# One router pass for both token tiles of a batch in the small experts of a four-layer model

## The reference

```python
logits = xf @ Wgate + expert_bias            # 8 experts
probs = jax.nn.softmax(logits, axis=-1)
topk_p, topk_i = jax.lax.top_k(probs, K)     # K = 2
topk_p = topk_p / jnp.sum(topk_p, axis=-1, keepdims=True)
comb = jnp.sum(jax.nn.one_hot(topk_i, E, dtype=xf.dtype) * topk_p[..., None], axis=1)
routed = jnp.einsum('ne,nec->nc', comb, _experts(xf, Wg, Wu, Wd))
return (shared + routed).reshape(b, t, c)
```

## Time and profile before

| | |
|---|---|
| time, median of 3 runs | 1422.37 us (1421.27 to 1424.42) |
| the profiled execution | 1424.82 us, span 1423.0 us |
| TensorE busy | 1323.8 us, 93% |
| VectorE busy | 1005.4 us, 71%, 1516 instructions |
| ScalarE busy | 871.2 us, 61% |
| POOL busy | 400.2 us, 28% |
| mean granted TensorE clock | 0.981 |

### The profile page before, as it was taken

How to read it: one execution, slowest core, us unless ns; L and a number is a source line. 1 busy time by engine, 2 the same in 40 slices (tenths; PEclk the granted TensorE clock), 3 DMA queues, 4 the chain that set the end, 5 groups by cost and what they waited for, 6 DMA issues and landing times.

```text
span 1423.0 us, 27091 instructions
## 1 busy us (share of the span) xinstructions
PE 1323.8 (93%) x10934; PEld 562.0 (39%) x10934; DVE 1005.4 (71%) x1516; ACT 871.2 (61%) x1104; POOL 400.2 (28%) x331
## 2 busy tenths in 40 slices
PE   7999998889879999999999998989998999999997
PEld 5344333333324444333444343433433334433443
DVE  3534777889925347698887868688868697978735
ACT  3334347788784454276566767666768676675672
POOL 5554430110011755452220223022305033202010
PEclk8999999999999999999999999999999999999998
DMA  6633101000001731011111010110010101100100
GB/s 177 118 62 70 25 14 31 16 2 2 2 1 39 196 60 34 1 32 24 35 24 24 1 23 1 24 35 10 15 24 1 23 13 24 31 13 19 24 1 15
DMA packets 30291, 45.80 MB, mean 32 GB/s; under 512 B 5892, under 2 KB 10692, under 8 KB 30116
## 3 DMA queue, kind: packets, MB, share of 16 engines
q1 hardware_dynamic: 30168, 44.08, 14.0%
HBM read 25.39 MB, written 1.18 MB: 19 GB/s over the span
## 4 chain that ended last, share of the span: by engine, by line
PE 72%; DVE 11%; ACT 8%; issue 4%; SPq 3%; DMA 2%; POOL 0%; ACTq 0%; DVEq 0%
PE ps L1264 13%; PE ps L1364 11%; PE ps L1309 7%; ACT PR L1442 6%; PE ps L1230 5%; PE ps L1250 5%; PE ps L1231 5%; PE ps L1232 5%; DVE BM L1530 3%; PE ps L1844 3%; PE ps L1328 2%; PE ps L1242 2%; PE ps L1271 2%; PE ps L1375 2%; PE ps L1324 1%
## 5 line engine op out<-in xcount | busy, mean ns | idle before, releaser
L1442 ACT ACTIVATE PR<-ps 128x1024 f32<-128x1024 f32 x432 | 431.2, 1026 | 207.1 <-PE ps L1271 136.4
L1530 DVE TENSOR_REDUCE BM<-ps 128x2 f32<-128x1024 f32 (+2 forms) x384 | 350.4, 950 | 57.0 <-PE ps L1250 55.9
L1264 PE MATMUL ps<-QS,KS 48*128 48x512 f16 (+7 forms) x2688 | 306.1, 329 | 31.7 <-ACT PR L1442 22.5
L1364 PE MATMUL ps<-PR,VS 128*32 128x512 f32 (+3 forms) x2304 | 231.5, 499 | 2.2 <-ACT PR L1442 1.6
L1264 PEld LDWEIGHTS ps<-QS,KS 48*128 48x128 f16 (+1 forms) x2688 | 108.5, 95 | 203.6 <-ACT PR L1442 88.5
L1250 PE MATMUL ps<-KS,QS 48*128 48x128 f16 (+2 forms) x1728 | 161.7, 273 | 19.2 <-DVE BM L1530 10.8
L1523 DVE TENSOR_REDUCE BM<-ps 128x8 f32<-128x1024 f32 x96 | 116.8, 1220 | 39.3 <-PE ps L1250 38.5
L1250 PEld LDWEIGHTS ps<-KS,QS 48*128 48x128 f16 x1728 | 68.0, 94 | 135.3 <-issue 45.8
L1571 POOL TENSOR_TENSOR OS<-OS,RX 128x512 f32<-128x512 f32 x24 | 30.5, 1270 | 273.9 <-ACT RX L1458 273.9
L1230 PE MATMUL ps<-YA,QS 128*128 128x512 f16 x256 | 99.6, 389 | 0.8 <-DVE RX L1489 0.5
L1231 PE MATMUL ps<-YA,QS 128*128 128x512 f16 x256 | 99.2, 388 | 0.0
(11 more groups left out here) (299 smaller groups left out, 2054.9 us busy)
## 6 DMA issues: line engine op xcount, KB each, us to landing
PR<-gates SPq DMA_DIRECT2D x32, 512.0 KB, 12.5
QS<-KS SPq DMA_DIRECT2D x64, 128.0 KB
QS<-KS SPq DMA_DIRECT2D x64, 64.0 KB
WM<-W_in SPq DMA_DIRECT2D x1, 2048.0 KB, 9.0
QS<-HL SPq DMA_DIRECT2D x48, 32.0 KB
KS<-HL SPq DMA_DIRECT2D x48, 32.0 KB
QS<-CT SPq DMA_DIRECT2D x96, 2.0 KB
KS<-KS SPq DMA_DIRECT2D x8, 128.0 KB, 2.4
```

Source lines behind the costliest of these rows:

```text
L1264: ins = pe.matmul(ps[pair][:, w, off:off + cols], KS[rows, ks, kt * P:(kt + 1) * P], QS[rows, qs, (ph + 1) * TT - cols:(ph + 1) * TT], sta ...
L1364: ins = pe.matmul(dst[32 * j:32 * j + 32, TT - cols:TT], v, PR[:, buf, j, off:off + cols], start=(g == 0), stop=(g == NGRP[ph] - 1))
L1442: act.activation(dst, src, ACT.Exp, scale=0.125 if lat else 1.0).then_inc(sig["exp"], 1)
L1530: ins = dve.tensor_reduce(BM[:, ph, p, :, qt - 4 * ph, part], bnk[:, :, off:off + nk * P], AX.X, ALU.max)
```

## The change

`routed(r, t)` says which tiles share a router: both of a batch, but for the second layer's batch 1 (r = 3, tiles 2 and 3), where each stays alone. `lg` now waits for the normalised rows of both tiles and issues 8 matmuls, the 22 steps and the exponential work on 64 columns (8 small ones), and only the transposes and all that follows stay a tile at a time. The step buffers move: six in `wq0`, four in `goon`, the bf16 parts in `gT`, the small columns in `ohb`, all of which an earlier router has left free. The planner's costs are 2.2 instead of 1.1 us for a shared `lg` and 0.23 instead of 0.20 us for a shared step. Five constants leave the priority tables with the values they had. The order of every engine in `Late` is laid out anew from these tasks with the same priorities.

```diff
         for t in (2 * b, 2 * b + 1):
             before = self.tile_before(r, t)
-            q = add("PE", f"lg{b}", ("lg", r, t), ("scl", kn, t), ("gtr",) + before if before else None)
-            for j in range(ROUTE):
-                x = add("DVE", f"rt{b}", ("rt", r, t, j), ("rt", r, t, j - 1) if j else q,
-                        ("rex", r, t) if j == 13 else None)
-                if j == 0:
-                    self.take(q, "misc", x)
-                if j == 2:
-                    add("ACT", f"rex{b}", ("rex", r, t), x)
-            q = add("PE", f"gtr{b}", ("gtr", r, t), x, ("gs",) + before + (1,) if before else None)
+            tiles = self.routed(r, t)
+            if t == tiles[0]:
+                x = add("PE", f"lg{b}", ("lg", r, t), *[("scl", kn, i) for i in tiles], ("gtr",) + before if before else None)
+                for j in range(ROUTE):
+                    q, x = x, add("DVE", f"rt{b}", ("rt", r, t, j), x, ("rex", r, t) if j == 13 else None)
+                    if j == 0:
+                        self.take(q, "misc", x)
+                    if j == 2:
+                        add("ACT", f"rex{b}", ("rex", r, t), x)
+                gates = x
+            q = add("PE", f"gtr{b}", ("gtr", r, t), gates, ("gs",) + before + (1,) if before else None)
...
+    def routed(r, t):
+
+        return (t,) if (r, t // 2) == (3, 1) else (t // 2 * 2, t // 2 * 2 + 1)
...
+        if task[0] in ("lg", "rt"):
+            n = len(self.routed(*task[1:3]))
+            return 1.1 * n if task[0] == "lg" else 0.17 + 0.03 * n
...
-        RTV = [wq0[:, :, :].rearrange("p n m -> p (n m)")[:, 32 * i:32 * i + 32] for i in range(10)]
-        RTB = wq0[:, :, :].rearrange("p n m -> p (n m)")[:, 320:368].bitcast(BF16).rearrange("p (i c) -> p i c", i=4)
+        RTV = ([wq0[:, :, :].rearrange("p n m -> p (n m)")[:, 64 * i:64 * i + 64] for i in range(6)]
+               + [goon[:, 64 * i:64 * i + 64] for i in range(4)])
+        RTB = gT[:, 0:96].bitcast(BF16).rearrange("p (i c) -> p i c", i=KT)
         GTB = rt_more[:, 0:256].bitcast(BF16)
-        RTM = [rt_more[:, 256 + 4 * i:256 + 4 * i + 4] for i in range(5)]
+        RTM = [ohb[:, :].bitcast(F32)[:, 8 * i:8 * i + 8] for i in range(5)]
...
-                    pe.wait_ge(sig["scl"], c("scl", 4 * (r - 1), t))
-                    for i in range(4):
+                    for i in range(4 * len(Late.routed(r, t))):
+                        if i % 4 == 0:
+                            pe.wait_ge(sig["scl"], c("scl", 4 * (r - 1), t + i // 4))
                         ins = pe.matmul(one[:, i * E:(i + 1) * E], XN[:, t * TT + i * P:t * TT + (i + 1) * P], w_rt1,
                                         start=True, stop=True)
...
-                    pe.wait_ge(sig["rt"], c("rt", r, t, ROUTE - 1))
+                    pe.wait_ge(sig["rt"], c("rt", r, Late.routed(r, t)[0], ROUTE - 1))
```

More of the change, by code:

```diff
@@ L265, in priority @@
         if kind == "sc":
-            v = None if scores >= w["scm"] else w["sc"] + w["sc1"] * scores
+            v = None if scores >= 2 else w["sc"] + w["sc1"] * scores
         elif kind == "un":
             lead = self.lead()
-            v = None if units >= w["unm"] or lead > w["leadm"] else (w["un0"] if lead <= w["lead"] else w["un2"]) + w["un1"] * units - w["une"] * (self.at["eu"][1] < 63)
+            v = None if units >= 2 or lead > 4 else (w["un0"] if lead <= w["lead"] else w["un2"]) + w["un1"] * units - w["une"] * (self.at["eu"][1] < 63)
         elif kind == "pv":
@@ L476 @@
              "SP": ("gd", "egb", "crow", "put", "kput", "st", "wl1", "wl2")}
[L477 to L480, removed]
+    WISH = {"sc": 2, "sc1": 1.02, "un0": 1.9, "un2": 2.1, "lead": 2, "un1": 1, "une": 1, "pv3": 2.5, "ahead": 3,
+            "pv": 3.61, "qk": 0.71, "vl": 1.9, "proj": 3.06, "ed": 1.1, "mean": 1, "eu": 1.2, "eu1": 0.3,
+            "mode": 0.4, "bldf": 0.8, "bld2": 3.31, "bld": 1.8, "up": 1.7, "dn": 1.22, "short": 1}
     def build(self):
@@ L681, in priority @@
                 first = task[1] in FAST
-                if (m > w["bldm"] and not first) or held >= (2 if first else 1):
+                if (m > 2 and not first) or held >= (2 if first else 1):
                     return None
@@ L686, in priority @@
                 held = sum(1 for x in self.held.values() if x[0] == "up")
-                return None if held >= w["upm"] and self.at["sc"][1] < 2 * NN - 1 else w["up"]
+                return None if held >= 2 and self.at["sc"][1] < 2 * NN - 1 else w["up"]
             return w["dn"] if kind in ("dn", "val") else w["short"]
@@ L1813, in pe_late @@
                     r, t = args
-                    pe.wait_ge(sig["rt"], c("rt", r, t, ROUTE - 1))
+                    pe.wait_ge(sig["rt"], c("rt", r, Late.routed(r, t)[0], ROUTE - 1))
                     pe.wait_ge(s_zero, ZERO[1] + 1)
                     for i in range(4):
-                        ins = pe.matmul(one[0:24, i * P:(i + 1) * P], RTB[:, i, :], onesb[:, :], start=True, stop=True)
+                        ins = pe.matmul(one[0:24, i * P:(i + 1) * P], RTB[:, 4 * (t - Late.routed(r, t)[0]) + i, :], onesb[:, :], start=True, stop=True)
                     ins.then_inc(sig["gtr"], 1)
@@ L1933, in act_late @@
                     act.wait_ge(sig["rt"], c("rt", r, t, 2))
-                    act.activation(RTV[1], RTV[0], ACT.Exp).then_inc(sig["rex"], 1)
+                    n = 4 * E * len(Late.routed(r, t))
+                    act.activation(RTV[1][:, 0:n], RTV[0][:, 0:n], ACT.Exp).then_inc(sig["rex"], 1)
                 elif kind == "gwh":
@@ L2002, in v3, with route, over_e @@
                 return x.rearrange("p (i e) -> p i e", e=E)
-            def over_e(x):
-                return x.unsqueeze(2).to_broadcast([P, 4, E])
-            first_choice = desc[:, :].unsqueeze(1).to_broadcast([P, 4, E])
-            def route(j, logits):
-                v = [v3(x) for x in RTV]
+            def route(j, logits, n):
+                def over_e(x):
+                    return x.unsqueeze(2).to_broadcast([P, n, E])
+                v = [v3(x[:, 0:n * E]) for x in RTV]
+                m = [x[:, 0:n] for x in RTM]
+                parts = RTB[:, 0:n, :]
+                first_choice = desc[:, :].unsqueeze(1).to_broadcast([P, n, E])
                 if j == 0:
-                    return dve.tensor_tensor(v[2], logits[:, 0:4 * E].rearrange("p (i e) -> p i e", e=E),
-                                             brow[:, :].unsqueeze(1).to_broadcast([P, 4, E]), ALU.add)
+                    return dve.tensor_tensor(v[2], logits[:, 0:n * E].rearrange("p (i e) -> p i e", e=E),
+                                             brow[:, :].unsqueeze(1).to_broadcast([P, n, E]), ALU.add)
                 if j == 1:
-                    return dve.tensor_reduce(RTM[0], v[2], AX.X, ALU.max)
+                    return dve.tensor_reduce(m[0], v[2], AX.X, ALU.max)
                 if j == 2:
-                    return dve.tensor_tensor(v[0], v[2], over_e(RTM[0]), ALU.subtract)
+                    return dve.tensor_tensor(v[0], v[2], over_e(m[0]), ALU.subtract)
                 if j == 3:
```

25 lines of the change are left out of this document (14 added, 11 removed), and 3 rows, old and new, of the table WISH.

## The result

The changed kernel took 1429.92 us (median of 12 executions, 1423.66 to 1432.55), the kernel before 1422.15 us beside it (12 executions, 1419.05 to 1429.04). The ratio is 1.0043, 95% interval 1.0025 to 1.0061: slower by 0.43%, where I had forecast 0.3% faster. The profiled execution took 1431.99 us, with a span of 1430.2 us.

A forecast was written before the change was run, and what follows sets the result against it. TensorE, busy 93%, was taken as the bound, so only its waits for VectorE counted: -6.0 + 2.2 = -3.8, about -4 us, from the median 1422.4 to 1418.4 us. The range was 1413 to 1427, the likeliest case 1416 to 1420.5.

The forecast's parts named there:

- 66 instructions, 12.1 us: VectorE's router instructions fall from 176 to 110; 66 removed at 0.184 us each, 12.1 us of busy time.
- The waits as the direct gain, -6.0: TensorE's waits for VectorE in three router windows (1.85, 1.84, 2.29 us), all taken as given back: -6.0 us.
- The widening, +2.2: The 66 router instructions in merged passes go from 32 to 64 columns, 34 ns each: at most 2.2 us added.
- The moved gates, 0 (between -4 and +4): Tile 0's gates and down projection, some 55 us later, fill idle time or displace attention: -4 to +4, taken as 0.
- The chain of the batch, 5.4 us late, covered: Tile 1's down projection ends 5.4 us later, puts 2.2 and 4.7 us late; cost 0, up to 6.9 if uncovered.
- the cover: Next quad's row of maxima is issued by 974.3, attention before it ends at 992.94: 18 us to hide late puts.
- Slower: Both tiles' gates meet in one bunch and the new order feeds TensorE worse: +5, 1427.4 us; chance 0.28.
- Its test: Idle and clock together, from router's start to second down projection, over 4 us more a batch than before.
- The order laid out anew: Planner's new order feeds TensorE worse around the gates: one more bad window +2, two +8; within Slower's 0.28.

The follow-up runs named there:

- e2_late: Kernel before, routers still separate, but tile 0's logits wait for tile 1's normalised rows in the three merged pairs, order laid out anew; ratio 1.0008.
- narrow form of the change: Changed kernel, same order and eight logits matmuls a pair, but a merged pass's steps and exponential work on tile 0's 32 columns alone; ratio 1.0006.
- draw: Kernel before, separate routers, with one planner cost altered so the order is laid out anew; three such kernels measured 1.0099, 1.0040 and 1.0161.
- pass in two halves: Changed kernel, same order, but each merged VectorE step issued as two of the old width, one a tile; ratio 1.0063, 1434.1 us.
- e7_merged_order_a: Changed kernel with only the planner's cost of a router step 0.01 larger, putting 526 TensorE tasks at another place; ratio 1.0006.

## Why the prediction was wrong, step by step

**66 instructions, 12.1 us.** Right: 1450 instead of 1516, 11.6 us less busy.

**The waits as the direct gain, -6.0.** This is the step that failed first. I took every wait of TensorE for VectorE in a window where a router runs as the router's doing. Leaving 54 steps out left the waits of all three windows where they were and gave +0.3 us (-3 to +4) at the order of before; at the late order +0.0006 against e2_late. The term was 0.

**The widening, +2.2.** The duration was right: 222 ns against 188 is the 34 ns that I worked out. The price was wrong by place. Charged in full it was still 2.2 us, as if time on VectorE were the most that it could cost. It cost nothing that can be told where a router stands early, about 5 us (1 to 9) at the change's order and about 10 (5 to 16) at the late one, there with four more logits matmuls a pair. All of the first and most of the second came as a lower granted clock of TensorE. In these two places a longer pass ahead of the gates was followed by more half-speed time; I had priced the wait and not what follows it. With 0 for the first term and 5 us for this one, my sum gives +5, near the measured +6.1 us (1.0043).

**The moved gates, 0 (between -4 and +4).** Right as a sum: 1.0008 with late gates alone. In the narrow form of the change, though, it is a balance: +6.2 us of rest and -5.8 of clock part, both clear of their errors (with late gates alone +3.8 and -1.9, the second not clear). The change so stands as late gates and a new order that cost some 6 us of stalls and would give as much back in clock, and a width that takes this back.

**The chain of the batch, 5.4 us late, covered.** Wrong in sign in two of the three batches, and without consequence: the merged pass started 3 us earlier than tile 1's router had and let tile 1's down projection begin at 820.98 instead of 827.53; in the second batch it began 1.7 us earlier, in the third 0.3 us later. The two puts went out 0.5 and 3.5 us later than before. TensorE's waits for transfers behind the first start are the same three as before, 1.1, 0.6 and 0.3 us, so the cover held.

**The rivals.** Slower had 0.28 and 1427.4 us, and is what came. Its mechanism was half right. Its test was more than 4 us more a batch in idle and clock, and it did not say which router's start it counts from. In 797 to 823 alone there are 2.63 idle + 5.2 clock = 7.8 us against 6.1, under the test. Over the whole stage, from where tile 0's router used to start, the three batches have 4.2, 4.0 and 5.6 us more, at or over it. The order laid out anew, the other half of that rival, can cost more than I gave it (up to 23 us in a draw), but in the change it did not, as the narrow kernel shows. The Trainium skill, page "Perfetto Trace Analysis", section "Optimizing Scalar/DVE Operations", says that where Scalar or Vector is not saturated but causes bubbles on other engines, breaking up instructions may allow work to be completed sooner. Its sign was right for the grouping at an order that stayed the same, which took 1.0008 to 1.0088; but breaking the steps of the merged pass up again, at the order of the change, brought nothing sooner (1.0063 against 1.0043).

**Left open.** Why some 0.6 us more of VectorE in a pass draws this much clock was not taken apart further, nor why the still longer pass in two halves draws none: the rows show that the clock falls after TensorE has been idle a little longer, not that this idle time is the cause of each fall. Nor is it settled whether merged routers are better or worse over many orders. No kernel here beats the one before; the merged one at another order (e7_merged_order_a, 1.0006) equals it.

## What to carry to other kernels

Before counting a wait as the gain of taking work off an engine, ask whether the wait would be there without that work: a reduction that starts when its input lands is waited for at any load. Where a hand-tuned or planned order is laid out anew, time two or three neighbouring orders of both kernels before a difference of a half per cent is put down to the change. And where a longer step stands on the path to a wait, look at the clock of the engine that waits and not at the step's own duration alone.

## What the runs showed of the hardware

- In these traces the clock falls in like portions of lost full-speed time. Cut in slices of 5 us from 620 us on, the profiled execution of the change has nine places where the granted clock is below full, of which seven lose 1.7 us, one 3.4 and one 5.2; the narrow one has six, of which four lose 1.7 and the others 3.4 and 5.2.
- Executions of one and the same kernel differ by 10 us and more (the kernel before 1417.03 to 1435.58 in one series), and with their clock: 1423.66 us at 0.984 and 1432.55 at 0.978 for the change. Taking the clock part out of the span left a rest that is steady to half a microsecond over 12 executions, and made differences visible that the medians blur.
- Dependent VectorE steps start 0.23 us apart at 32 columns and 0.26 at 64.
